# Normalised rows made by ScalarE instead of GpSimd, and the scatters' gates moved, in an attention and mixture-of-experts kernel

## The reference

```python
def _layernorm(x, axis=-1, eps=1e-05):
    m = jnp.mean(x, axis=axis, keepdims=True)
    v = jnp.var(x, axis=axis, keepdims=True)
    return (x - m) / jnp.sqrt(v + eps)

# x, ctx: (128, 128, 256) f32; 16 heads of 16; no affine part in the layernorms
x = x + xattn(_layernorm(x), ctx, ctx, Wq, Wk, Wv, Wo)   # softmax(q k^T / sqrt(16)) v, then Wo
h = _layernorm(x)                                        # one row of 256 for each of 16384 tokens
shared = sum over 2 experts of gelu(h @ up^T) @ down^T
probs  = softmax(h @ router_w.T); the top 4 of 16 experts, weighted by their probability
x = x + shared + sum over the 4 chosen experts of p * (gelu(h @ up_e^T) @ down_e^T)
```

## Time and profile before

| | us |
|---|---|
| median of three runs | 3096.67 |
| the profiled execution, its time | 3078.89 |
| its span (first to last instruction) | 3077.1 |
| busy PE, DVE, ACT, POOL | 2219.2, 1683.0, 974.5, 1843.3 |

### The profile page before, as it was taken

One profiled execution on the slowest core, in us unless ns is written; L12 is line 12 of the kernel. 1 busy time (PEld: TensorE's weight loads), 2 busy tenths in 40 slices (PEclk: granted clock), 3 DMA queues, 4 the chain that ended last, 5 costly groups with the idle time before them and its releaser, 6 DMA issues.

```text
span 3077.1 us, 55896 instructions
## 1 busy us (share of the span) xinstructions
PE 2219.2 (72%) x21056; PEld 1713.7 (56%) x21056; DVE 1683.0 (55%) x4681; ACT 974.5 (32%) x1826; POOL 1843.3 (60%) x1716
## 2 busy tenths in 40 slices
PE   6888888888888888888886299999994333334331
PEld 3655556556565656655654288888894233323321
DVE  3555555554555555545554288888873544454444
ACT  2433333333333333433332155555551010101100
POOL 2355555545555555555544566666657777777776
PEclk8999988888889999999996599999997666666665
DMA  4223232222222232222222377777784555455543
GB/s 171 67 71 104 73 98 72 89 86 87 87 74 94 70 98 79 92 83 83 83 73 69 123 277 274 275 276 276 275 296 147 154 164 156 149 159 160 154 128 119
DMA packets 207370, 420.50 MB, mean 137 GB/s; under 512 B 25601, under 2 KB 124929, under 8 KB 207106
## 3 DMA queue, kind: packets, MB, share of 16 engines
q1 hardware_dynamic: 157954, 282.65, 27.5%
q0 software_dynamic: 49152, 134.28, 13.4%
HBM read 215.50 MB, written 201.33 MB: 135 GB/s over the span
## 4 chain that ended last, share of the span: by engine, by line
PE 39%; POOL 20%; DVE 17%; issue 9%; another core or an unknown queue 9%; ACT 6%; DMA 1%; POOLq 0%; DVEq 0%; SPq 0%; ACTq 0%
POOL gb L1004 19%; PE A L382 5%; PE A L355 5%; PE A L433 4%; PE A L450 4%; PE A L549 4%; PE A L533 3%; ACT pr L593 3%; PE A L472 3%; DVE mx L682 3%; PE A L437 3%; DVE xl L866 3%; PE A L516 3%; PE A L465 2%
## 5 line engine op out<-in xcount | busy, mean ns | idle before, releaser
L967 POOL DMA_INDIRECT xs<-xn,idx x512 | 502.1, 981 | 695.5 <-PE A L450 305.5
L1004 POOL DMA_INDIRECT gb<-ys,idx x512 | 587.6, 1148 | 174.3 <-issue 174.3
L516 PE MATMUL A<-ident,xr 128*128 128x128 f32 x1408 | 209.7, 298 | 472.7 <-DVE xl L866 421.4
L516 PEld LDWEIGHTS A<-ident,xr 128*128 128x128 f32 x1408 | 180.2, 154 | 512.8 <-issue 446.0
L593 ACT ACTIVATE pr<-A 128x512 f32<-128x512 f32 x512 | 264.4, 603 | 551.7 <-PE A L437 280.6
L900 DVE SCALAR_TENSOR_TENSOR ob<-gb,gw,ob 128x256 f32<-128x256 f32 x512 | 205.6, 479 | 416.3 <-DMA gb<-ys,idx 404.0
L682 DVE TENSOR_REDUCE mx<-A 128x4 f32<-128x512 f32 x512 | 316.7, 680 | 178.3 <-remote 125.8
L615 ACT ACTIVATE xh<-A 128x512 fp32r<-128x512 f32 x352 | 194.0, 599 | 365.9 <-PE A L516 198.6
L621 ACT ACTIVATE act<-A 128x512 f32<-128x512 f32 x208 | 124.2, 598 | 528.3 <-PE A L533 261.9
L989 POOL TENSOR_TENSOR hl<-act,hh 128x512 fp32r<-128x512 f32 x144 | 187.2, 1300 | 146.8 <-DVE hh L871 146.8
L549 PE MATMUL A<-wt,hh 128*128 128x256 f32 x1152 | 241.7, 293 | 0.0
(11 more groups left out here) (158 smaller groups left out, 4616.8 us busy)
## 6 DMA issues: line engine op xcount, KB each, us to landing
xr<-xs SPq DMA_DIRECT2D x144, 512.0 KB
ys<-yo SPq DMA_DIRECT2D x144, 512.0 KB, 3.9
xb<-in_x SPq DMA_DIRECT2D x32, 512.0 KB
cg<-in_ctx_t SPq DMA_DIRECT2D x32, 512.0 KB
yd<-xb SPq DMA_DIRECT2D x32, 512.0 KB, 3.1
x2d<-xn SPq DMA_DIRECT2D x32, 512.0 KB, 3.3
xr<-x2d SPq DMA_DIRECT2D x32, 512.0 KB
yr<-yd SPq DMA_DIRECT2D x32, 512.0 KB
```

The lines of the kernel that those rows point to most:

```text
L516: ins = tr(banks[c][:, q * P:(q + 1) * P], xr[t % 3][:, q, c * P:(c + 1) * P], ident[:, :])
L967: q.indirect_dma_start(xs, bass.IndirectOffsetOnAxis(ap=idx[:, n, k:k + 1], axis=0), x2[g % 4][:, i, :], None).then_inc(sent[g % 4], 16)
L1004: q.indirect_dma_start(gb[p][:, i, k, :], None, ys, bass.IndirectOffsetOnAxis(ap=idx[:, n, k:k + 1], axis=0)).then_inc(got[p], 16)
```

## The change

Three things are changed. First, the eight tiles of normalised rows of a group are made by ACT, as scale * x + bias with scale = rs and bias = -mean * rs; POOL makes only these small tiles (128 x 4), with two more instructions for each layernorm (`ng`, `nb`). The new steps on ACT are NA1 (at position 2, between ACT's `osb` and `ot`; for the first two groups at the start) and NA2 (at position 0 of the next group, between `ot` and the exponentials). Second, the gates of a batch's four scatters are S(n), PV(n-1), OTR(n-1) and OT(n-1), in place of S(n), PV(n), OT(n), OP(n). Third, the places of the scatters in the list move a little, which on POOL, whose only other steps are LN1 and LN2, changes nothing in its order. LN1 and LN2 keep their places on POOL.

```diff
--- before.py
+++ after.py
@@ -37,8 +37,8 @@
 
 def attention_steps():
 
-    out = [("LN1", 0), ("XT", 0), ("K0", 0), ("K1", 0), ("Q0", 0), ("Q1", 0), ("VA", 0), ("VB", 0), ("VA", 1), ("VB", 1),
-           ("LN1", 1), ("XT", 1), ("S", 0), ("MT", 0), ("ST", 0)]
+    out = [("LN1", 0), ("NA1", 0), ("XT", 0), ("K0", 0), ("K1", 0), ("Q0", 0), ("Q1", 0), ("VA", 0), ("VB", 0), ("VA", 1), ("VB", 1),
+           ("LN1", 1), ("NA1", 1), ("XT", 1), ("S", 0), ("MT", 0), ("ST", 0)]
     for n in range(B):
         g, i = divmod(n, GT)
         first, second, third, after = {
@@ -47,11 +47,16 @@
             2: (("VA", 2 * g + 2), ("VB", 2 * g + 2), ("RL", g - 1), []),
             3: (("VA", 2 * g + 3), ("VB", 2 * g + 3), ("XT", g + 2), [("LN2", g), ("R1", g - 1), ("WS", g)])}[i]
         s = TOPK * (n - 2 * GT - 1)
-        out += [("S", n + 1), ("SC", s), first, ("PV", n), ("SC", s + 1), second, ("OTR", n), ("MT", n + 1), ("OT", n),
-                ("SC", s + 2), third, ("OP", n), ("SC", s + 3), ("ST", n + 1)]
+        out += [("S", n + 1), ("SC", s), first, ("PV", n), ("SC", s + 1)]
+        if i == 2:
+            out.append(("NA1", g + 2))
+        out += [second, ("OTR", n), ("SC", s + 2), ("MT", n + 1), ("OT", n), ("SC", s + 3)]
+        if i == 0:
+            out.append(("NA2", g - 1))
+        out += [third, ("OP", n), ("ST", n + 1)]
         out += after
     g = G
-    out += [("RK", g - 2), ("R2", g - 2), ("XT2", g - 1), ("RL", g - 1), ("R1", g - 1), ("RK", g - 1), ("R2", g - 1)]
+    out += [("RK", g - 2), ("R2", g - 2), ("NA2", g - 1), ("XT2", g - 1), ("RL", g - 1), ("R1", g - 1), ("RK", g - 1), ("R2", g - 1)]
     out += [("SC", k) for k in range(TOPK * (B - 2 * GT - 1), TOPK * B)]
     last = {"SC": TOPK * B, "S": B, "MT": B, "ST": B, "VA": 2 * G, "VB": 2 * G}
     return [(name, n) for name, n in out if 0 <= n < last.get(name, B if name in ("PV", "OTR", "OT", "OP") else G)]
@@ -156,6 +161,7 @@
         t32 = sa("t32", [P, KC, T])
         stage = [sa(f"stage{k}", [P, 1, 2, E]) for k in range(2)]
         st1, mv1, ve1, rs1 = sa("st1", [P, GT, 6]), sa("mv1", [P, GT, 2]), sa("ve1", [P, GT]), sa("rs1", [P, GT])
+        ng1, nb1, ng2, nb2 = (sa(k, [P, GT]) for k in ("ng1", "nb1", "ng2", "nb2"))
         st2, mv2, ve2, rs2 = sa("st2", [P, GT, 6]), sa("mv2", [P, GT, 2]), sa("ve2", [P, GT]), sa("rs2", [P, GT])
         lmax, ls, ex = sa("lmax", [P, GT]), sa("ls", [P, GT, NRT]), sa("ex", [P, GT, NRT])
         rsum, rrec = sa("rsum", [P, GT]), sa("rrec", [P, GT])
@@ -203,6 +209,7 @@
         fill = [sem(f"fill{b}") for b in range(8)]
         drain = [sem(f"drain{b}") for b in range(8)]
         ln1_st, ln1_mv, ln1_ve, ln1_rs, xn_ready = sem("ln1_st"), sem("ln1_mv"), sem("ln1_ve"), sem("ln1_rs"), sem("xn_ready")
+        ln1_pw, ln2_pw = sem("ln1_pw"), sem("ln2_pw")
         m_hi, m_lo = sem("m_hi"), sem("m_lo")
         rd_ready, y_ready = sem("rd_ready"), sem("y_ready")
         ln2_st, ln2_mv, ln2_ve, ln2_rs, xn2_ready = sem("ln2_st"), sem("ln2_mv"), sem("ln2_ve"), sem("ln2_rs"), sem("xn2_ready")
@@ -606,8 +613,27 @@
                 wait(act_e, r1, 6 * g)
                 ac(ex[:, :, :], ls[:, :, :], ACT.Exp).then_inc(r_exp, 1)
 
+            def NA1(g):
+                act_e.wait_ge(ln1_rs, g + 1)
+                if g > 0:
+                    wait_filled(act_e, 1, "XT", g - 1)
+                    wait_filled(act_e, 2, "XT", g - 1)
+                for i in range(GT):
+                    ac(xn[:, i, :], xb[g % 4][:, i, :], ACT.Identity, bias=nb1[:, i:i + 1], scale=rs1[:, i:i + 1])\
+                        .then_inc(xn_ready, 1)
+
+            def NA2(g):
+                act_e.wait_ge(ln2_rs, g + 1)
+                wait(act_e, sent[g % 4], 16 * TOPK * GT * (g // 4))
+                wait(act_e, x2_kept[g % 4], 16 * (g // 4))
+                if g == 3:
+                    act_e.wait_ge(zeroed, 16 * NRT)
+                for i in range(GT):
+                    ac(x2[g % 4][:, i, :], xb[g % 4][:, i, :], ACT.Identity, bias=nb2[:, i:i + 1], scale=rs2[:, i:i + 1])\
+                        .then_inc(xn2_ready, 1)
+
             act_e.wait_ge(const_set, 1)
-            run(ATT, {"K0": K0, "K1": K1, "Q0": Q0, "Q1": Q1, "XT": XT, "XT2": XT2, "ST": ST, "PV": PV, "OT": OT, "R1": R1})
+            run(ATT, {"NA1": NA1, "NA2": NA2, "K0": K0, "K1": K1, "Q0": Q0, "Q1": Q1, "XT": XT, "XT2": XT2, "ST": ST, "PV": PV, "OT": OT, "R1": R1})
 
             def TR(t):
                 for c in range(KC):
@@ -659,7 +685,7 @@
                     ins = v.bn_stats(st1[:, i, :], xb[g % 4][:, i, :])
                 ins.then_inc(ln1_st, 1)
                 dve.wait_ge(ln1_st, g + 1)
-                wait(dve, xn_ready, GT * g)
+                wait(dve, ln1_rs, g)
                 for i in range(GT):
                     ins = v.bn_aggr(mv1[:, i, :], st1[:, i, :])
                 ins.then_inc(ln1_mv, 1)
@@ -709,7 +735,7 @@
 
             def LN2(g):
                 dve.wait_ge(y_ready, GT * (g + 1))
-                wait(dve, xn2_ready, GT * g)
+                wait(dve, ln2_rs, g)
                 for i in range(GT):
                     ins = v.bn_aggr(mv2[:, i, :], st2[:, i, :])
                 ins.then_inc(ln2_mv, 1)
@@ -927,30 +953,23 @@
 
             def LN1(g):
                 pool.wait_ge(ln1_mv, g + 1)
+                wait(pool, xn_ready, GT * g)
                 q.tensor_scalar(ve1[:, :], mv1[:, :, 1], EPS, None, ALU.add).then_inc(ln1_ve, 1)
-                pool.wait_ge(ln1_ve, g + 1)
-                q.tensor_tensor(rs1[:, :], ve1[:, :], neg_half[:, :], ALU.pow).then_inc(ln1_rs, 1)
-                pool.wait_ge(ln1_rs, g + 1)
-                if g > 0:
-                    wait_filled(pool, 1, "XT", g - 1)
-                    wait_filled(pool, 2, "XT", g - 1)
-                for i in range(GT):
-                    q.tensor_scalar(xn[:, i, :], xb[g % 4][:, i, :], mv1[:, i, 0:1], rs1[:, i:i + 1],
-                                    ALU.subtract, ALU.mult).then_inc(xn_ready, 1)
+                q.tensor_scalar(ng1[:, :], mv1[:, :, 0], -1.0, None, ALU.mult).then_inc(ln1_ve, 1)
+                pool.wait_ge(ln1_ve, 2 * (g + 1))
+                q.tensor_tensor(rs1[:, :], ve1[:, :], neg_half[:, :], ALU.pow).then_inc(ln1_pw, 1)
+                pool.wait_ge(ln1_pw, g + 1)
+                q.tensor_tensor(nb1[:, :], ng1[:, :], rs1[:, :], ALU.mult).then_inc(ln1_rs, 1)
 
             def LN2(g):
                 pool.wait_ge(ln2_mv, g + 1)
+                wait(pool, xn2_ready, GT * g)
                 q.tensor_scalar(ve2[:, :], mv2[:, :, 1], EPS, None, ALU.add).then_inc(ln2_ve, 1)
-                pool.wait_ge(ln2_ve, g + 1)
-                q.tensor_tensor(rs2[:, :], ve2[:, :], neg_half[:, :], ALU.pow).then_inc(ln2_rs, 1)
-                pool.wait_ge(ln2_rs, g + 1)
-                wait(pool, sent[g % 4], 16 * TOPK * GT * (g // 4))
-                wait(pool, x2_kept[g % 4], 16 * (g // 4))
-                if g == 3:
-                    pool.wait_ge(zeroed, 16 * NRT)
-                for i in range(GT):
-                    q.tensor_scalar(x2[g % 4][:, i, :], xb[g % 4][:, i, :], mv2[:, i, 0:1], rs2[:, i:i + 1],
-                                    ALU.subtract, ALU.mult).then_inc(xn2_ready, 1)
+                q.tensor_scalar(ng2[:, :], mv2[:, :, 0], -1.0, None, ALU.mult).then_inc(ln2_ve, 1)
+                pool.wait_ge(ln2_ve, 2 * (g + 1))
+                q.tensor_tensor(rs2[:, :], ve2[:, :], neg_half[:, :], ALU.pow).then_inc(ln2_pw, 1)
+                pool.wait_ge(ln2_pw, g + 1)
+                q.tensor_tensor(nb2[:, :], ng2[:, :], rs2[:, :], ALU.mult).then_inc(ln2_rs, 1)
 
             def SC(s):
 
@@ -962,7 +981,7 @@
                 pool.wait_ge(xn2_ready, GT * (g + 1))
                 at = n + 2 * GT + 1
                 if at < B:
-                    b, stage_of, m = ((3, "S", at), (5, "PV", at), (7, "OT", at), (0, "OP", at))[k]
+                    b, stage_of, m = ((3, "S", at), (5, "PV", at - 1), (7, "OTR", at - 1), (7, "OT", at - 1))[k]
                     wait_filled(pool, b, stage_of, m)
                 q.indirect_dma_start(xs, bass.IndirectOffsetOnAxis(ap=idx[:, n, k:k + 1], axis=0),
                                      x2[g % 4][:, i, :], None).then_inc(sent[g % 4], 16)
```

## The result

The changed kernel is slower: 3175.11 us (median; 3169.31 to 3177.25) against 3099.11 us, ratio 1.0239 [1.0209, 1.0268], +76 us. The forecast was 3066 us and its range ended at 3132.

What follows compares the result with a forecast made beforehand. It took runs of scatters holding ST's fill, until 1.45 to 1.9 us after the last starts, as the bound. Terms -7.5 - 17.4 - 15.4 - 16.5 + 34 - 8.4 = -31 us took 3096.7 to 3066 us; range 3014 to 3132.

Steps and rivals of the forecast that it cites:

- a fill of ST that falls into a scatter: Positions 2 and 3: such a fill is held until about 1.45 us after the scatter's start, or a run's last.
- -16.5 + 34: Position 0: ten iterations (n = 84 to 120) gain 1.65 us each; eighteen (n = 12 to 80) lose 1.9 us each.
- rival C: PV is held like ST, by LN2's run at position 0 and the index run at position 1: +41 us, 3107; chance 0.16.
- the shift of -0.55 us: Positions 1 and 2: the eighth scatter behind LN1 starts at 170.1 against 170.66; times 28, -15.4 us.
- the 0.62 us: Position 3: no scatter left, 0.74 us less at ST, 0.12 given back for S(n+2) leading less; times 28, -17.4 us.
- ScalarE's rows: Positions 2 and 0: four row tiles on ACT take 1.9 us (bounds 1.2 and 2.7), in idle time, costing nothing.
- -7.5: Start and tail: 1.0 us gained for group 0, 2.3 for group 1, 4.2 in the tail; bounds -3 and -10 us.
- the slow iterations: Position 0, n = 12 to 80, clock 0.50 during ST: ST's fill passes, S's is held to 9.65 us; +1.9 us each.
- rival A: Position 0: ST's fill in the 18 slow iterations is held too; +3.6 us each, +65 us, 3131 us; chance 0.27.
- rival B: Only ST is ever held and S passes; the 18 gain 1.1 us instead of losing 1.9: -54 us, 3012; chance 0.14.
- the 8.4 us: Last two groups: without LN1, scatters at positions 1 and 2 stay clear of ST; 2.1 us four times, -8.4 us.
- D: The holding has another cause than scatters; only start and tail are gained: 3089 us; chance 0.04.

Runs made afterwards that it cites:

- pv_at_0_1: The changed kernel with only the eight scatters of positions 0 and 1 gated on PV's fill of their own iteration; 3059.5 us, 0.9885 of the kernel before.

## Why the prediction was wrong

**What bounds the kernel: right in kind, too narrow.** That runs of scatters hold PE, and for how long behind the last one, held up (1.87 and 1.90 us for the V product in the rows above, 2.77 us for ST at position 2). Wrong was whom they hold. The reading "a fill of ST that falls into a scatter" came from the dense stages on which scatters lay in the kernel before, ST and the S behind it (whose maxima waited 125.8 us for "remote"); the V product had none on it, which is no evidence that it is immune.

**The step that failed: position 0.** Its term, -16.5 + 34, put LN2's run on the V product and charged nothing. That was rival C, which I gave 0.16 and priced at 1.3 us here and 2.8 us at position 1, in ten groups. Measured: the copy 4.2 us later on the mean (in 28 of the 29 groups; the last has no run on it), 2.5 us of it hidden, and a clock of 0.50 that now lies on OP and ST of all groups (7.08 us an iteration against 2.88), which I had only for half of the slow ones: +1.46 x 29 = +42 us against +17.5. In position 1 the index run makes the V product's copy 2.2 us later, by holding S's fill, the Q projection or the V product itself; ST's clear end gives 0.75 back: +1.18 x 29 = +34 us. `pv_at_0_1` shows the cause: with both gone the kernel is 1.1% faster than before. That its 3060 us are near the forecast's 3066 is chance: position 2's loss is still in it, and position 0 is 1.3 us an iteration faster than before instead of slower.

**Also failed: position 2.** Eight scatters in a row, the last starting 6.90 us after `ot`; the shift of -0.55 us was 0.3 the other way, and behind it another 0.9 us came from ST's matmuls no longer starting ahead of the run: +1.24 x 29 = +36 us, not -15.

**Right.** Position 3 has the idle time of 1.37 us; its period gained only 0.34 of the 0.62 us: S(n+2) leads less (behind the run of eight it starts at 1111.84, with the exponentials at 1112.10), and 0.7 us more goes by before `osb`. ScalarE's rows took 0.59 us each and 2.06 us for four, and `ot` still waited 0.23 us for PE behind them: nothing on the path, as said, though I took 1.9 us. The estimate from the Trainium skill (ScalarE: Activation LUTs, What ACT_TABLE_LOAD costs) was just these 2.06 us, so the trace agrees with it. POOL's extra instructions took 0.23 and 0.20 us. The start gained 4.4 us, and the tail 6 us from the last exponentials to its first scatter, -10 in place of -7.5. But the second phase, taken as unchanged, was 4 us longer (1335 against 1331 us from its first `wt`).

**In the slow iterations** ST's fill passed as forecast, 0.5 us into the first scatter, so rival A was wrong. S's fill passed in 5 of 29 groups, where the second scatter came 2.5 us after the first; in the other 24 it was held as forecast, but by 0.9 to 2.0 us and not to the run's end, and the rest of the run lay on the Q projection and the V product. So rival B, that S passes, was wrong as well. The last two groups gained nothing of the 8.4 us (n = 120 to 127: +3 us), as their scatters ran together too.

**Sum.** Forecast -31; the profiled executions +98: 42 + 34 + 36 - 10 for the four positions from n = 12 on, -3 ahead of n = 12 (the start's 4.4 us, a part of it lost again) and -2 behind the last exponentials (6 gained, 4 lost), which is 98 before rounding. Two slips in the prediction's own figures changed nothing: D's 3089 us is no slower, yet its chance stands with "slower", and the range begins at 3014 though B gives 3012. Without its gates the change would have been 119 us faster than before: the half on ScalarE's rows was sound, and the gates undid it.

## What to carry to other kernels

An immunity that was never exposed is no immunity: before moving work past a stage, ask whether the trace has a single case of the two side by side, and if not, price the hold as for the stage where it is seen. Indirect transfers issued in a run did least harm beside PE's sparse stages (a few full matmuls or transposes a us), when no dense stage ran beside the same run before them. The gate was one event ahead of that window by the queue's own delay (0.8 us from the fill to the first scatter's start here). A gate that is always past does not spread work, it collects it into a run. And one iteration shown in full is not the typical one until its neighbours have been compared: the 2.5 us gap of n = 77 is there in 5 groups of 29.
